# The adapter stage with its inputs laid out by the host, keys in banks of their own, a filler on TensorE, and its end in another order

## What is computed

```
enc = ctx[:, :73]; ca = ctx[:, 73:]                # 77 context rows of 96, the last 4 are tokens
hs     = mha(x @ Wq, enc @ Wk, enc @ Wv)           # 8 heads of 20
ca_q1  = (ca^T @ Wq_ca)[:, indices]                # 96 distinct rows, repeated to 512
ca_hs1 = mha(ca_q1, x, x)
ca_hs2 = mha(ca_hs1 @ Wq, ca @ Wk_ca, ca @ Wv_ca)
x      = (hs + ca_hs2) @ Wout + b_out + x
```

## Time and profile before

| | before |
|---|---|
| median of 3 runs | 1027.56 us |
| profiled execution | 1029.73 us |
| its span | 1027.9 us |
| PE busy | 978.5 us, 95% |
| DVE, ACT, POOL busy | 690.7, 591.1, 378.9 us |
| hardware DMA queue | 16.52 MB, 6.4% of 16 engines |

### The profile page before, as it was taken

How to read it: one execution, slowest core, us unless ns; L and a number is a source line. 1 busy time by engine, 2 the same in 40 slices (tenths; PEclk the granted TensorE clock), 3 DMA queues, 4 the chain that set the end, 5 groups by cost and what they waited for, 6 DMA issues and landing times.

```text
span 1027.9 us, 17534 instructions
## 1 busy us (share of the span) xinstructions
PE 978.5 (95%) x6376; PEld 706.1 (69%) x6376; DVE 690.7 (67%) x1171; ACT 591.1 (57%) x1332; POOL 378.9 (37%) x493
## 2 busy tenths in 40 slices
PE   7999978999999999999999999999999989999998
PEld 4566666656667666667666668666556689998887
DVE  2767646776774676774777674776645789999463
ACT  2666635667763766764666764666644455455442
POOL 2676623344342434332444332343321034444120
PEclk9999989999999999999999999999999999999999
DMA  6400050000000000000000000000000330000000
GB/s 135 94 1 1 1 148 1 1 1 2 1 1 2 1 1 2 1 1 1 1 1 2 1 1 2 1 1 2 1 1 25 100 95 1 1 1 1 1 26 26
DMA packets 25371, 17.64 MB, mean 17 GB/s; under 512 B 8566, under 2 KB 24102, under 8 KB 25286
## 3 DMA queue, kind: packets, MB, share of 16 engines
q1 hardware_dynamic: 25285, 16.52, 6.4%
HBM read 11.26 MB, written 1.31 MB: 12 GB/s over the span
## 4 chain that ended last, share of the span: by engine, by line
PE 64%; DVE 10%; ACT 5%; issue 4%; POOL 1%; DMA 1%; SPq 0%; DVEq 0%; ACTq 0%; POOLq 0%
PE banks L409 13%; PE banks L396 12%; PE banks L382 11%; PE banks L416 4%; PE banks L224 3%; ACT sa_probs L499 3%; PE banks L1645 2%; PE banks L227 2%; PE banks L226 2%; PE banks L225 2%; PE banks L1937 2%; DVE ca_top L1780 2%; PE banks L232 2%; DVE ca_probs L1785 1%; DVE sa_negmax L571 1%
## 5 line engine op out<-in xcount | busy, mean ns | idle before, releaser
L643 POOL TENSOR_SCALAR sa_probs<-sa_probs,sa_inverse 128x512 f32<-128x512 f32 x320 | 216.8, 692 | 361.7 <-DVE sa_inverse L575 361.7
L499 ACT ACTIVATE sa_probs<-banks,sa_negmax 128x512 f32<-128x512 f32 x320 | 215.6, 685 | 125.7 <-DVE sa_negmax L571 125.6
L571 DVE TENSOR_REDUCE sa_negmax<-banks 128x2 f32<-128x1024 f32 x160 | 188.7, 1218 | 10.4 <-PE banks L382 7.4
L396 PEld LDWEIGHTS banks<-ident,sa_probs 128*128 128x128 f32 x1280 | 144.5, 141 | 55.6 <-issue 27.6
L396 PE MATMUL banks<-ident,sa_probs 128*128 128x128 f32 x1280 | 172.6, 275 | 9.9 <-ACT sa_turned L510 5.8
L580 DVE COPY sa_turned<-banks 128x512 f32<-128x512 f32 x160 | 110.1, 688 | 75.6 <-PE banks L396 75.6
L409 PE MATMUL banks<-sa_turned,sa_v 128*64 128x512 f32 x640 | 155.0, 605 | 0.0
L382 PE MATMUL banks<-sa_k_parts,sa_q_parts 64*128 64x512 f32 x960 | 133.2, 408 | 1.9 <-ACT sa_probs L499 1.9
L510 ACT COPY sa_turned<-banks 128x512 f32<-128x512 f32 x160 | 94.2, 589 | 58.2 <-PE banks L396 56.3
L382 PEld LDWEIGHTS banks<-sa_k_parts,sa_q_parts 64*128 64x128 f32 x960 | 83.9, 184 | 30.4 <-issue 14.1
L409 PEld LDWEIGHTS banks<-sa_turned,sa_v 128*64 128x64 f32 x640 | 38.7, 136 | 74.3 <-issue 73.1
(11 more groups left out here) (218 smaller groups left out, 1727.2 us busy)
## 6 DMA issues: line engine op xcount, KB each, us to landing
w_o<-in_L_xattn_wo SPq DMA_DIRECT2D x2, 800.0 KB, 9.1
out<-x SPq DMA_DIRECT2D x4, 320.0 KB, 2.4
w_q_t<-in_L_xattn_wq_t SPq DMA_DIRECT2D x1, 1120.0 KB, 10.4
fold_values<-ca_turned SPq DMA_DIRECT2D x5, 192.5 KB
x<-in_x SPq DMA_DIRECT2D x1, 960.0 KB, 5.8
fold_values<-ca_probs SPq DMA_DIRECT2D x4, 192.5 KB
w_q_t<-in_L_xattn_wq SPq DMA_DIRECT2D x1, 640.0 KB, 6.2
w_o<-in_L_xattn_wk SPq DMA_DIRECT2D x1, 640.0 KB, 9.2
```

The lines of the kernel that those rows point to most:

```text
L396: last = pe.transpose(b_turn[e][:, q * P:(q + 1) * P], probs[:, j % 2, e, q, k * P:(k + 1) * P], ident[:])
L499: act.activation(probs[:, j % 2, e, q, :], b_scores[u % 2][:, e, :], ACT.Exp, bias=negmax[:, u % RING, e:e + 1], accum_out=total[:, u % RI ...
L571: dve.tensor_reduce(negmax[:, u % RING, :], b_scores[u % 2], AX_X, ALU.max, negate=True).then_inc(s_max.sem, 1)
L643: pool.tensor_scalar(probs[:, j % 2, e, q, :], probs[:, j % 2, e, q, :], inverse[:, u % RING, e:e + 1], 1.0, ALU.mult, ALU.mult).then_inc( ...
```

## The change

- The host gives x turned (`x_turned`), x padded by head (`x_padded`), the context turned, the tokens apart, and the weights padded. The kernel loads these; `turn_x`, `copy_x`, `pad_x`, the transposes of the context, and the clearing of the weight tiles are gone. x turned and padded for batches 2 and 3 is loaded within the loop as its buffers come free.
- The order of the loads is new, with a semaphore for each thing waited for.
- Keys and token values go to banks 4 and 7 (`b_keys`), apart from the scores' pair; `scores1(0)` no longer waits for their copies. `max1(0)` comes ahead of the token values' spreading on DVE.
- PE begins with three matmuls of 512 columns on a tile set to 1.0 (`keep_busy`), whose result nobody reads.
- The small vectors of the second layer come as one array (`constants`), one DMA in place of 22.
- The end: `expand_probs2` of the last batch stands ahead of `project_out(11)` in slot 18; ACT does the exp2 ahead of the norm's scaling and the copy of the expanded probabilities ahead of its rounding; DVE's remainder is moved from slot 17 to slot 18, behind `update(11)`.

```diff
 of_slot
-        out = [("x", 0, g) for g in range(G)] + [("queries", 0, g) for g in range(G)] if s == 0 else []
+        out = [("queries", 0, g) for g in range(G)] if s == 0 else []
-        if k == 0 and b + 1 < B:
-            out += [("x", b + 1, g) for g in range(G)]
 adapter
+        b_keys = (banks[4], banks[7])
 SP
+            sp.dma_start(flat(tokens[:]), flat(t["tokens"])).then_inc(s_tokens, 16)
+            sp.dma_start(flat(wq_ca[:]), t["wq_ca"]).then_inc(s_tokens, 16)
+            sp.dma_start(w_ctx[:, 0:3, :, :].rearrange("p w h c -> p (w h c)"), flat(t["w_ctx"][:, 0:3, :])).then_inc(s_w, 16)
+            sp.dma_start(flat(ctx_t[:]), t["ctx_turned"]).then_inc(s_w, 16)
+            turned_x(0)
+            sp.dma_start(wq[:].rearrange("p g h c -> p (g h c)"), t["wq_padded"]).then_inc(s_wq, 16)
+            sp.dma_start(own[:], t["own"]).then_inc(s_own, 16)
+            sp.dma_start(flat(wv), t["w_ctx"][:, 3, :]).then_inc(s_wv, 16)
+            sp.dma_start(ident[:], t["ident"]).then_inc(s_ident, 16)
+            padded_x(0)
+            sp.dma_start(flat(wo[:]), t["wo_padded"]).then_inc(s_wo, 16)
             sp.dma_start(b_o[:], w("b_out").unsqueeze(0).broadcast_to([P, D])).then_inc(s_wo, 16)
             sp.dma_start(expand[:], t["expand"]).then_inc(s_wo, 16)
+            sp.dma_start(x[:], tiles).then_inc(s_x_in, 16)
+            split_weights(0)
+            turned_x(1)
+            split_weights(1)
+            padded_x(1)
+            split_weights(2)
+            padded_x(2)
             for tile, src in later:
                 sp.dma_start(tile, src).then_inc(s_later, 16)
+            for b in range(2, B):
+                sp.wait_ge(s_s1.sem, s_s1.at((b - 2) * NP + NP - 1, 0))
+                ring.wait_made(sp, ("queries", b - 2, 1))
+                turned_x(b)
+                if b >= 3:
+                    sp.wait_ge(s_pv1.sem, s_pv1.at(b - 3, 1))
+                    padded_x(b)
 PE
-            for g in range(G):
-                turn_x(0, g)
+            def keep_busy(n):
+                for _ in range(n):
+                    pe.matmul(b_out, turned[:, 0, 0:P], turned[:, 0, :], start=True, stop=True)
+
+            pe.wait_ge(s_busy, 1)
+            keep_busy(WARM)
...
                 if k == 1 and 1 <= b <= B:
                     project_hs1(b - 1)
+                if s == NU + 2:
+                    expand_probs2(B - 1)
                 if 0 <= s - OUT_LAG < NU - 3:
                     project_out(s - OUT_LAG)
...
-                if k == 0 and b + 1 < B:
-                    turn_x(b + 1, 0)
-                    turn_x(b + 1, 1)
 ACT
                 if s == NU + 1:
+                    exp2(B - 1)
                     act.wait_ge(s_later, 16 * len(later))
-                    next_ln.scale_and_round(act, 0, banks[0:2], lambda eng: None)
+                    next_ln.scale(act, 0, banks[0:2])
+                    copy_expanded(B - 1)
+                    next_ln.round(act, 0, lambda eng: None)
 DVE
-            dve.memset(x_pad[:], 0.0).then_inc(s_zero_pad, 1)
+            dve.memset(turned[:, 0, :], 1.0).then_inc(s_busy, 1)
...
-                if s == NU + 1:
+                if s == NU + 2:
                     next_ln.remainder(dve, 0, lambda eng: None)
```

More of the change, by code:

```diff
@@ L754, in adapter @@
         wo = sb("wo", [P, G, D])
-        wk, wv, wk_ca, wv_ca = (sb(n, [CTX, H0, HP]) for n in ("wk", "wv", "wk_ca", "wv_ca"))
+        w_ctx = sb("w_ctx", [CTX, 4, H0, HP])
+        wk, wk_ca, wv_ca, wv = (w_ctx[:, i, :, :] for i in range(4))
         wq_ca = sb("wq_ca", [NCA, H0, HP])
@@ L855, in _ @@
-            sp.dma_start(x[:, 0:QT, :], tiles[:, 0:QT, :]).then_inc(s_in, 16)
-            sp.dma_start(own[:], t["own"]).then_inc(s_w, 16)
-            sp.wait_ge(s_zero, 5)
-            for tile, name in ((wq_ca, "Wq_ca"), (wk, "Wk"), (wk_ca, "Wk_ca"), (wv_ca, "Wv_ca"), (wv, "Wv")):
-                sp.dma_start(tile[:, :, 0:HD0], by_head(w(name))).then_inc(s_w, 16)
-            sp.wait_ge(s_zero, 7)
-            for h in range(H0):
-                sp.dma_start(wq[to(h), h // HG, :, 0:HD0], by_head(w("Wq")[h * HD0:(h + 1) * HD0, :])).then_inc(s_wq, 16)
@@ L863, in _, with turned_x, padded_x @@
-            sp.dma_start(x[:, QT:, :], tiles[:, QT:, :]).then_inc(s_xrest, 16)
-            for h in range(H0):
-                sp.dma_start(wo[to(h), h // HG, :], w("Wout")[h * HD0:(h + 1) * HD0, :]).then_inc(s_wo, 16)
+            def turned_x(b):
+                sp.dma_start(x_t[:, b % 2, :, :], t["x_turned"][b, :, :, :]).then_inc(s_xt[b], 16)
+            def padded_x(b):
+                sp.dma_start(flat(x_pad[:, b % 3, :, :, :].rearrange("p q h c -> p q (h c)")), flat(t["x_padded"][b, :, :, :])).then_inc(s_xpad[b], 16)
@@ L1022, in project_out @@
                 pe.matmul(out_of(u), turned_end[:, b % 2, q, :], folded[:, b % 2, CH - 1, :], start=False, stop=True).then_inc(s_o.sem, 1)
[L1024 to L1031 removed]
+            def keep_busy(n):
[3 more added lines that the diff above has]
+            keep_busy(WARM)
+            pe.wait_ge(s_tokens, 32)
             for g in range(G):
@@ L1045, in _ @@
                 project_queries(0, g)
-            for g, bank in enumerate((b_out, b_token)):
-                pe.matmul(bank[:, 0:NK], flat(wv[:, g * HG:(g + 1) * HG, :]), ctx_t[:, :, 0:SE], start=True, stop=True).then_inc(s_vp.sem, 1)
+            pe.wait_ge(s_wv, 16)
+            for g in range(G):
+                last = pe.matmul(b_small[:, g, 0:NK], flat(wv[:, g * HG:(g + 1) * HG, :]), ctx_t[:, :, 0:SE], start=True, stop=True)
+            last.then_inc(s_vp.sem, 1)
             for s in range(SLOTS):
@@ L1125, in copy_queries @@
                 act.activation(q_t[:, b % 2, g, :], ring.bank(banks, item), ACT.Copy, scale=SCALE0).then_inc(ring.s_act, 1)
-            def copy_x(b):
-                item = ("x", b, 0)
-                ring.wait_made(act, item)
-                if b >= 2:
-                    act.wait_ge(s_s1.sem, s_s1.at((b - 2) * NP + NP - 1, 0))
-                    ring.wait_made(act, ("queries", b - 2, 1))
-                act.copy(x_t[:, b % 2, 0, :], ring.bank(banks, item)).then_inc(ring.s_act, 1)
             def copy_hs1(b):
@@ L1167, in _ @@
                 copy_queries(0, g)
-            for i, bank in enumerate((b_out, b_token)):
-                act.wait_ge(s_vp.sem, s_vp.at(0, i))
-                act.copy(v_all[:, i, :], bank[:, 0:NK]).then_inc(s_v.sem, 1)
+            act.wait_ge(s_vp.sem, s_vp.at(0, 0))
+            act.copy(v_all[:], b_small[:, :, 0:NK]).then_inc(s_v.sem, 1)
             for s in range(SLOTS):
@@ L1346, in _ @@
             next_ln.start_gpsimd(pool)
-            for tile in (wq_ca, wk, wk_ca, wv, wv_ca, wq, wo):
-                pool.memset(tile[:], 0.0).then_inc(s_zero, 1)
-            pool.memset(v_diag[:], 0.0).then_inc(s_zero, 1)
-            pool.wait_ge(s_zero, 8)
+            pool.memset(v_diag[:], 0.0).then_inc(s_zero_values, 1)
+            pool.wait_ge(s_zero_values, 1)
             each = lambda ap: ap.unsqueeze(2)
```

160 lines of the change are left out of this document (70 added, 90 removed).

## The result

| | before | changed |
|---|---|---|
| median of the runs on one chip | 1027.72 us | 1018.67 us (1015.68 to 1019.88, 4 runs) |
| ratio | | 0.9906, interval 0.9881 to 0.9931 |
| profiled execution, its span | 1029.73, 1027.9 us | 1019.83, 1018.0 us |
| PE busy | 978.5 us | 974.7 us |
| DVE, ACT, POOL busy | 690.7, 591.1, 378.9 us | 683.6, 588.9, 377.5 us |

The kernel is faster, by 9.1 us. The forecast was 1014.0 in a range of 1010.2 to 1019.8: the sign and the range held, the middle was 4.7 us too low. By the profiled executions 13.6 us were forecast and 9.9 came.

The account below looks back on a forecast made before the run. PE was taken to bound mid-adapter, with a low clock at the start and waits at the end. Gains 7.0 + 1.4 + 5.2 = 13.6 us off 1029.73 gave 1016.1, less the profile's offset 1014.0 us; range 1010.2 to 1019.8.

Parts of the forecast that it names:

- Term 1: Adapter's start: `project_queries(1, 0)` begins at 21.4 us instead of 28.43, when x turned of batch 1 lands; gain 7.0 us.
- The formula of the Trainium skill: Load of x turned: bytes / 436 GB/s behind 2.0 us, so landing at 15.9 us and a gain of 9.6 us.
- the rival held at 0.08: Slot 1: the clock falls in PE's wait for x turned, price 1.9 and 1 us more: 1017 us; chance 0.08.
- The first rival: Start: the filler does not bring the clock up in time, slot 1 at 25.0 us: 1017.6 us; chance 0.26.
- Term 2: Slots 4 and 8: eight transposes each removed from PE, 0.8 and 0.6 us gained, 1.4 us in all.
- the copies were worth nothing: Slots 4 and 8: padding copies and ACT copies worth nothing, since DVE and ACT wait for PE there.
- The new loads of x turned cost nothing in the loop: Batch 2's load, issued near 30 us, used near 45, costs nothing; rival of late loads near 1045 us, chance 0.04.
- Term 3: Adapter's end: token softmax and expansion start earlier, last update at 152.8 us against 158.06; gain 5.2 us.
- the clock should stay up: Adapter's end: PE idles under 1 us at a time, so its output tiles should keep the upper clock.
- All that follows keeps its time.: Behind the adapter: instructions are kept, so it was taken as unchanged, at no gain or loss.
- a change of the second layer's length by over 1 us: Second layer: a length changed by over 1 us was listed as a sign that the forecast is wrong.
- the offset of 2.2 us: Whole kernel: the profiled execution lies 2.2 us above the median, so 1016.1 us profiled became 1014.0 for the runs.

Follow-up runs that it names:

- end_old: The changed kernel with the adapter's end in the order of before, all else as changed: median 1019.06 us, ratio 0.9922.
- ballast: The changed kernel with eight transposes of the identity put back on PE in slots 4 and 8: median 1015.66 us, ratio 0.9873.
- dve_ballast: The changed kernel with one memset of 128x640 on DVE in slots 4 and 8: median 1019.33 us, ratio 0.9909.
- before_end_new: The kernel before with the new order of the adapter's end alone: median 1023.42 us, ratio 0.9961.
- x_early: The changed kernel with x turned of batch 1 loaded behind ident, ahead of padded x of batch 0: median 1014.58 us, ratio 0.9856.

## Why the prediction was right, and what it missed

**Term 1, the start (7.0 us).** The mechanism holds: the clock was up behind the filler, PE's own way was done at 18.1 us (18.8 forecast; the filler began at 1.55 and not at 2.05 us and took 4.56 and not 5.2, since the clock rose within it), and x turned of batch 1 came last, at 21.92 (21.4 forecast). 6.5 us were gained at that point. The filler had little part in it: without it the gain there is 6.1 us. What let the load land so late was not its bytes alone: SP could not issue it before 13.30 us. The mean over the windows from 3 to 22 us is 309 GB/s, near the 300 of the forecast's 5.35 MB in 17.8 us; so the estimate came out through its mean, which is luck in part: the forecast had no term for SP being held, and single microseconds reached 419 GB/s. The formula of the Trainium skill (DMA: Bandwidth & Descriptors, Anatomy of one DMA) had, by the forecast's estimate from it, the load land at 15.9 us; its 436 GB/s was nearly reached for a microsecond, never held, and the measurement decides for 21.8.

**The step that failed in term 1** is the rival held at 0.08, that the clock falls in slot 1's wait. It was set aside because the wait would be 2.6 us and not 3.1. It was 3.83, and the clock fell in both profiled executions of this program in which it had stayed up until then. In three of the experiments with the same start (end_old, ballast, dve_ballast) it fell at 10 us instead, in the keys' small matmuls; then PE came to slot 1 at 22 us without any wait. Either way slot 1 begins its queries near 22 us; the fall in the wait costs 1.7 us more (scores at 25.5 against 23.8). The first rival was priced too high: it put slot 1 at 25.0 us with a clock that never comes up in the filler, and even the version without filler had PE ready there at 21.2. The two rivals, clock not held by small matmuls (0.26) and clock falling in the wait, were in truth the two outcomes of one program, and together deserved well over the 0.34 they had; and the forecast should have looked on for the same at the hand-over.

**Term 2, slots 4 and 8 (1.4 us).** 0.76 and 0.60 us came in these two slots, and 1.92 up to slot 15. The number holds and the path does not. The working made PE's transposes the path and said that the copies were worth nothing, because DVE and ACT wait for PE in those slots. In the trace of before the copy stands directly ahead of the next slot's max, with no idle time between:

```profile
50.40 0.68 DVE L1227 COPY ad_x_t<-banks 128x512 f32<-128x512 f32 x1
51.16 1.22 DVE L1232 TENSOR_REDUCE ad_negmax<-banks 96x2 f32<-96x1024 f32 x1
```

DVE's time put back moves that max at once (0.68 and 0.67 us), the transposes move it by 0.02; these act in later slots, 0.62 us in all. The step read the wait of the slot's first instruction on DVE for that of its last. A right sum hid a wrong path, so this hit is luck. What the copies on ACT and the padding copies were worth was not tested. The new loads of x turned cost nothing in the loop, as said: `project_queries(2, 0)` and `(3, 0)` begin at 48.52 and 78.42 us with no idle time of PE ahead of them.

**Term 3, the end (5.2 us).** 5.54 us in the profile, near the upper bound of 5.6, the same 5.54 with the end's edit alone (16.32 to 10.78), and 5.53 lost again with the old end (16.31). The output tiles ran at one pace, with one wait of 0.57 us among them. The mechanism holds. Its remark that the clock should stay up because PE idles for under 1 us at a time held here, but is no rule: with the memset on DVE the clock fell in slot 14 behind 0.74 us.

**"All that follows keeps its time."** This failed, by 2.7 us, more than any term; a change of the second layer's length by over 1 us was one of the forecast's own signs of being wrong. The instructions there are the same. The clock is not (1.6 and 1.7 us lost), nor is one wait of the execution before (0.9 us gained). The idle time at the hand-over is 1.99 us before and 2.05 after. Before, the clock had been down from 148 to 155 us and no fall followed the hand-over; after, it fell in 1.3 us. `end_old`, with its own low stretch just before, has no fall at the hand-over either, and `before_end_new`, without one, has it. So part of what term 3 gains by avoiding a low stretch is taken back by the next wait. In both profiles with the hand-over filler it is gone; that the filler does so by shortening the idle time, rather than by one more 512-column matmul, was not separated. What started the stretch at 820 us is open: its idle time of 0.70 us (0.72 before, without a fall) does not tell the two apart.

**The number.** By the table, 4.8 us of term 1 were left behind the slow queries, 0.4 came before slot 4's max (no run tells from what), then 1.9 and 5.5: 12.6 in place of 13.6. With the 2.7 lost later, 1029.73 - 12.6 + 2.7 = 1019.8 us, the profiled execution. For the median, the offset of 2.2 us below the profiled run was carried over from before, where the wait at 808 us makes 0.9 of it; after, it was 1.2 in the first job and 3.6 in the second, where the slower runs are those with the lower mean clock.

## What to carry to other kernels

A wait that is removed at one place may only move the instant at which the chip grants TensorE its lower clock: when costing an edit, list every idle time of PE that it leaves, those behind the edited code too, and put a price on each, here 1.6 to 1.8 us. Work taken off before a transfer lands is worth nothing until the transfer is moved: look first at when SP could issue it, not only at its bytes. And to price a removed instruction, look at what stands directly behind it on its own engine; a busy share or a wait at the head of the slot does not tell. Shares from two experiments that each put one thing back need not add up to the whole, even where the sum seems to fit.

## What the runs showed of the hardware

- **One program has several clock histories.** With the same start, the clock fell at 10 us in three profiled executions and at 22 us in two. Medians of one program differed by 2.7 us between two jobs (1018.67 and 1015.93), each with its own ratio to before (0.9906 and 0.9891). The fall at 10 us costs nothing at the end, because slot 1 waits for its load anyway; the one at 22 us costs 1.7 us.
- **The lower clock came in stretches of two lengths** in all thirteen profiles, apart from the ones that the program's end cuts short: 3.4 us, or 6.8 us (148.1 to 154.9 before; at the start and at the old end in the experiments). A stretch of 3.4 us in dense work cost 1.6 to 1.8 us.
- **The same hand-over decides by what preceded it**: with about 2 us of idle PE and the full clock until then, the clock fell in nine profiles of nine; just behind another low stretch (before, `end_old`) and with 1.50 us of idle and a filler (two profiles) it did not.
- **Small matmuls did not always hold the clock** that a filler of three 512-column ones had brought up: it fell in the keys in four profiled executions with that filler (`x_early` among them). Two more 512-column matmuls among them held it, in both profiles that had them.
- **SP's issue of a DMA can block**: 4.50 us for one 640 KB load at 7.20 us, against 0.42 for one of 512 KB. What stands behind it in the program is late by that. It was held so in all eleven profiles of the new start, for 4.5 to 5.6 us. Busy DMA engines alone don't explain it: at 13.77 us another load of 640 KB was issued in 0.43 us with their share at 1.14. What holds SP is open.
- **The clock column of the windows reads 1.00 at the start** while 512-column records take 0.77 us in place of 0.46 (6.14 us for 8 in the version without filler, 3.70 after). The durations tell the pace there, not the column. The trace's own clock record begins only at 5.04 us after and at 16.17 us in the version without filler, where the durations shorten; ahead of that it has no entry.
